# A graph network on one core: the first attention's weight product and its single-column vectors computed in two steps, with new hand-written orders

## The chip, the cores and the metric

The kernel runs on one core of one Trainium2 chip. The metric is the device time of one launch in microseconds (us); lower is better. The core's engines are PE (TensorE, matrix products), DVE (VectorE), ACT (ScalarE), POOL (GpSimd) and SP (SyncE, which only starts transfers). They run side by side, and each executes its own list of instructions strictly in order.

## The reference

Sixty-four graphs of 128 nodes with 256 features pass through four residual layers, each followed by a layer normalization:

```python
x = layernorm(x + attention(x, adj))      # L0: weight = adj * exp(q k^T), rows divided by their sums, times v
x = layernorm(x + gcn3(x, adj))           # L1: three times adj @ (x @ W) + b, relu after the first two
x = layernorm(x + hypergraph(x, adj))     # L2: up to 512, relu, layer norm, down to 256; H = (adj != 0)
x = layernorm(x + heads8(x, adj))         # L3: 8 heads, scores times 2*adj, softmax, Wo
```

Only the setup of L0 is changed. With q = x Wq^T + bq and k = x Wk^T + bk, the scores need, up to terms that the division by the row sums removes, the matrix Wq^T Wk, the vectors Wk^T bq and Wq^T bk, and the number bq . bk.

## The kernel before

**Groups.** Four graphs make a group; there are 16 groups. Each layer of a group is cut into named steps on each engine. For instance `att_t` multiplies the combined matrix "att" with the transposed input `xT`, `att_v0` and `att_v1` make the values, `att_scores` the scores, `att_exp` the exponentials, `att_turn` transposes them, and `att_out` multiplies with the values.

**The orders.** What runs when is written out by hand, in three tables with one list per engine. `PROLOGUE` fills the pipeline with groups 0 to 2. `SCHEDULE` is the loop, twelve iterations; in it, stage A is attention and GCN of group t, stage B the end of the GCN and the hypergraph layer of group t-1, stage C the eight heads of group t-2. `EPILOGUE` drains groups 13 to 15. Semaphores between the engines keep every order correct; an order only decides how long an engine stands at a wait. `keep_busy` steps on PE are four products of 512 columns whose result nobody reads.

**Split weights.** Every weight of a single-pass product is split by ACT into a rounded part (`high_W...`, line 978) and by DVE into what is left (`rest_W...`, line 1056: the weight minus its rounded part, both in SBUF). The input is split in the same way: `x_high` on ACT (line 906), `x_rest` on POOL (line 1382). All matrix products are recorded on line 476; one in full precision makes two records.

**The setup of L0.** `set_att` on PE waits for the biases and `Wq0`, `Wk0`. For each half m of the rows it makes the product (4 records of 256 columns) and behind it two vectors (8 records of one column); at the end comes bq . bk (4 records). Only then does it signal `att_mm`. `set_att` on DVE waits for that and for `Wv0T`, copies everything out of PSUM, and signals `att_ready`. ACT makes `high_att` from it, DVE `rest_att`, and PE's `att_t` waits for `rest_att`. `att_v0` waits for `rest_Wv0T`, whose last two columns hold one of the vectors. `att_t` on ACT adds the vector `t0`.

**Behind it on PE.** In `PROLOGUE`, `set_down` (16 records; waits for the transfer of `WdownT` and for DVE's `set_reps`) stands ahead of `att_t`, with two `keep_busy` steps ahead of it. DVE's `set_down` folds a gain into `WdownT`; ACT's `high_WdownT` waits for it.

**Transfers.** SP issues thirteen at the start: biases, `Wq0` and `Wk0`, `xT`, `Wv0T`, adjacency, x, rows, transposed adjacency, `W1` and `W2`, `W3` to `WoT`, `WdownT` (line 431), `WupT` with `Wqk3T` (line 432), and the adjacency once more.

**Steps of the loop that matter here.** `gram` on PE waits for the four sums `res0` that DVE's `att_out` and `att_res1` make. `hyper_down0` and `hyper_down1` on PE end with transposes of `sqs` (line 715), which DVE's `square_sum0` and `square_sum1` (lines 1216 to 1223) make. `z2_rest0` and `z2_rest1` on DVE (line 1147) subtract after ACT's `gcn_2a`. `hyper_out` on PE multiplies `y2`, which DVE makes in `hyper_y0` and `hyper_y1` (line 1228) after a power on POOL.

Of the kernel before, what the change touches and what calls it, by code (L numbers as in the profile page):

```python
# [1438 lines left out]
```

## Time and profile before

| | us |
|---|---|
| median of 3 runs | 1061.04 (1059.98 to 1061.5) |
| the profiled execution, its own time | 1061.14 |
| its span, first to last instruction | 1059.4 |
| mean granted clock of TensorE, share of full speed | 0.995 |

The profile is one execution. Durations are those of its records; "start" counts from the first instruction. In a list by time a row reads: start, length, engine, line, operation, output<-inputs, shapes, number of records merged in the row, and in brackets how long the engine had been idle and what ended that. PEld is the loading of weights into PE, which overlaps its products.

### The profile page before, as it was taken

Reading aid. Unit: us, or ns where it says so; the run is one execution under the profiler, and the core shown is the slowest. Engines: PE = TensorE matmul, PEld = TensorE weight load, DVE = VectorE, ACT = ScalarE, POOL = GpSimd, SP = SyncE. Lnnn points to the kernel's source line nnn. Section 1 sums busy time; section 2 is a strip of 40 time slices with the busy share of each in tenths; the row PEclk is TensorE's granted clock in tenths of the full one; section 3 lists DMA queues with packets and bytes.
Section 4 is the critical chain, followed back from the end, with each engine's and each line's share of the span. In section 5 each row is a group of like instructions: output and inputs, shape, how many; then the busy total and the mean of one; then the engine's idle time right before and its main releaser. Section 6 shows DMA issues by size and latency. Waiting matters only on the chain.

```text
span 1059.4 us, 21720 instructions
## 1 busy us (share of the span) xinstructions
PE 1026.7 (97%) x8376; PEld 913.4 (86%) x8376; DVE 839.8 (79%) x2247; ACT 654.5 (62%) x1755; POOL 485.2 (46%) x298
## 2 busy tenths in 40 slices
PE   8899999999999999999999999999999999998876
PEld 7688898898989889898988889898988989897764
DVE  4666878878797888879788887978888797978566
ACT  3444855839475683948568394856839485673724
POOL 2315363745435364543536464353546445351613
PEclk9999999999999999999999999999999999999998
DMA  6110101011110101111010111101011110000001
GB/s 228 50 61 9 62 2 61 21 41 51 33 59 21 51 21 41 51 41 50 22 50 22 40 51 41 51 21 50 31 32 51 41 51 21 32 2 11 21 1 40
DMA packets 17383, 43.35 MB, mean 41 GB/s; under 512 B 2048, under 2 KB 2048, under 8 KB 17152
## 3 DMA queue, kind: packets, MB, share of 16 engines
q1 hardware_dynamic: 17280, 41.97, 11.8%
q8 instruction: 66, 1.08, 0.4%
q14 instruction: 37, 0.30, 0.1%
HBM read 33.57 MB, written 8.39 MB: 40 GB/s over the span
## 4 chain that ended last, share of the span: by engine, by line
PE 92%; ACT 3%; DVE 3%; issue 1%; POOL 0%; DMA 0%; POOLq 0%; SPq 0%; DVEq 0%
PE ps L476 83%; PE ps L788 5%; PE ps L729 1%; ACT pr L948 1%; PE ps L579 1%; PE ps L715 1%; DVE pr L1245 1%; PE ps L659 1%; DMA pr<-in_weights 0%; DVE mx L1250 0%; DVE st L1067 0%; DVE aT_rest L1147 0%; ACT aT_high L885 0%; POOL rstd L1331 0%; ACT up_high L925 0%
## 5 line engine op out<-in xcount | busy, mean ns | idle before, releaser
L948 ACT ACTIVATE pr<-pr,mx 128x128 f32<-128x128 f32 x384 | 149.4, 407 | 9.6 <-DVE mx L1250 9.6
L1377 POOL TENSOR_TENSOR pr<-pr,den 128x1024 f32<-128x1024 f32 x64 | 122.1, 1916 | 56.6 <-DVE den L1265 56.6
L1331 POOL TENSOR_TENSOR rstd<-var,neg_half 128x4 f32<-128x4 f32 (+1 forms) x84 | 73.5, 876 | 143.9 <-DVE var L1078 143.9
L1083 DVE TENSOR_SCALAR x<-x,mv,rstd 128x256 f32<-128x256 f32 x256 | 90.6, 417 | 38.8 <-POOL rstd L1331 38.0
L1356 POOL TENSOR_TENSOR x<-x,rows 128x1024 f32<-128x1024 f32 x16 | 38.1, 2381 | 178.6 <-PE ps L476 178.6
L1067 DVE BATCH_NORM_STATS2 st<-x 128x6 f32<-128x256 f32 x256 | 91.6, 415 | 0.7
L1361 POOL TENSOR_TENSOR up_rest<-upT,up_high 128x1024 fp32r<-128x1024 f32 x32 | 81.9, 2561 | 0.0
L1245 DVE TENSOR_TENSOR pr<-ps,adjB 128x1024 f32<-128x1024 f32 x64 | 75.2, 1218 | 7.3 <-PE ps L476 7.3
L948 ACT ACTIVATION_READ_ACCUMULATOR pr<-pr,mx 128x1 f32 x384 | 79.1, 206 | 0.0
L902 ACT COPY s_s<-ps 128x512 f32<-128x512 f32 x32 | 18.8, 587 | 95.2 <-PE ps L476 95.2
L1250 DVE TENSOR_REDUCE mx<-pr 128x8 f32<-128x1024 f32 x64 | 76.4, 1201 | 0.0
L942 ACT ACTIVATE qkT<-ps,biases 128x512 f32<-128x512 f32 x64 | 42.2, 688 | 55.1 <-PE ps L476 54.9
L476 PE MATMUL ps<-W_high,aT_high 128*128 128x256 f32 x256 | 69.9, 298 | 1.9 <-ACT aT_high L885 1.9
L788 PE MATMUL ps<-ident,pr 128*128 128x128 f32 x512 | 67.6, 275 | 3.8 <-POOL pr L1377 1.9
L1366 POOL TENSOR_TENSOR hv<-hv,neg_half 128x2 f32<-128x2 f32 x32 | 22.4, 701 | 103.6 <-DVE hv L1211 103.6
L476 PE MATMUL ps<-W_rest,aT_high 128*128 128x256 f32 x256 | 65.6, 281 | 0.0
L788 PEld LDWEIGHTS ps<-ident,pr 128*128 128x128 f32 x512 | 57.5, 142 | 8.7 <-issue 5.7
L476 PE MATMUL ps<-WdownT_high,up_high 128*128 128x258 f32 x256 | 64.3, 283 | 0.0
L476 PE MATMUL ps<-WdownT_rest,up_high 128*128 128x258 f32 x256 | 63.9, 282 | 0.0
L1269 DVE COPY pr<-ps 128x512 f32<-128x512 f32 x64 | 43.5, 679 | 17.3 <-PE ps L788 17.0
L1350 POOL TENSOR_TENSOR x<-x,rows 128x1024 f32<-128x1024 f32 x16 | 38.6, 2413 | 38.7 <-PE ps L476 38.7
L1147 DVE TENSOR_TENSOR aT_rest<-ps,aT_high 128x512 fp32r<-128x512 f32 x64 | 41.7, 676 | 17.7 <-ACT ps L898 10.9
(199 smaller groups left out, 3310.7 us busy)
## 6 DMA issues: line engine op xcount, KB each, us to landing
xT<-in_xT SPq DMA_DIRECT2D x16, 512.0 KB, 3.7
x<-in_x SPq DMA_DIRECT2D x16, 512.0 KB, 3.3
out_x<-x SPq DMA_DIRECT2D x32, 256.0 KB, 2.1
adjA<-in_adj SPq DMA_DIRECT2D x16, 256.0 KB, 2.7
adjTA<-in_adjT SPq DMA_DIRECT2D x16, 256.0 KB, 2.7
adjB<-in_adj SPq DMA_DIRECT2D x16, 256.0 KB, 2.9
pr<-in_weights SPq DMA_DIRECT2D x2, 512.0 KB, 6.0
qkT<-in_weights SPq DMA_DIRECT2D x1, 1024.0 KB, 12.1
```

Of the source, the lines that this page charges most:

```text
L476: return pe.matmul(out, lhsT, rhs, start=(k == 0), stop=(k == n - 1))
L788: last = pe.transpose(ps4[:, turn_bank(b) + k // 4, k % 4], pr[:, b, k, :], ident[:])
L942: act.activation(qkT[:, m, :], ps[:, 4 + m, :], ACT.Identity, bias=b_qk[:, m, :], scale=ATT if m < C else 1.0).then_inc(qk_ready, 1)
L948: act.activation(pr[:, b, k, :], pr[:, b, k, :], ACT.Exp, bias=mx[:, b, k:k + 1], accum_out=den[:, b, 0, k:k + 1]).then_inc(exp_ready, 1)
L1067: dve.bn_stats(st[i][:, b, :], t[:, b, :]).then_inc(norm_step[i], 1)
L1083: dve.tensor_scalar(t[:, b, :], t[:, b, :], mv[i][:, b, 0:1], rstd[i][:, b:b + 1], ALU.subtract, ALU.mult).then_inc(ready, 1)
L1245: dve.tensor_tensor(pr[:, b].rearrange("p (j i) n -> p j i n", i=C), ps4[:, 4:8, 2 * bb:2 * bb + 2, :], mask, ALU.mult).then_inc(masked_re ...
L1250: dve.tensor_reduce(mx[:, b, :], pr[:, b], AX.X, ALU.max, negate=True).then_inc(mx_ready, 1)
L1269: dve.tensor_copy(pr[:, b, 4:8, :], ps4[:, turn_bank(b) + 1]).then_inc(prT_dve, 1)
L1331: pool.tensor_tensor(rstd[i][:, bs], var[i][:, bs], neg_half[:, bs], ALU.pow).then_inc(rstd_ready[i], len(pairs))
L1361: pool.tensor_tensor(up_rest[:, fs, :], upT[:, fs, :], up_high[:, fs, :], ALU.subtract).then_inc(up_rest_ready, 1)
L1377: pool.tensor_tensor(pr[:, b], pr[:, b], den[:, b, 1, :].unsqueeze(2).broadcast_to([P, HEADS, P]), ALU.mult).then_inc(pr_ready, 1)
```

## The change

1. **Two steps on PE.** `set_att` now makes only the two halves of the product and signals `att_mm` after each half. A new step `set_vec` makes the 20 single-column records, all into one bank of PSUM, and signals `vec_mm`.
2. **Two steps on DVE.** `set_att` copies each half when it is there (`att_ready` counts to 2). `set_vec` copies `t0` (now one copy of two columns), `c0` and the two columns of `Wv0T`, and signals `vec_ready`. `high_att` waits for `att_ready`; `high_Wv0T` and ACT's first `att_t` wait for `vec_ready`.
3. **Orders of the prologue.** ACT: `x_high` first, then `high_att`, `high_Wv0T`, `att_v0`; the other roundings later. PE: both first `keep_busy` ahead of `set_att`, `att_t` directly behind `set_vec`, `set_down` behind `att_v0`. DVE: `rest_att` and `rest_Wv0T` ahead of `set_reps`, `rest_W1` and `rest_W3` behind `gram_scale`, `rest_WoT` and `rest_Wqk3T` behind group 0. POOL: `x_rest0` ahead of `att_t` (the addition of the value bias to x).
4. **Orders of loop and epilogue.** Many neighbours change places on every engine. In all, PE has 5 instead of 7 `keep_busy` steps in the prologue and 12 instead of 10 in the epilogue.

```diff
 PROLOGUE = {
-    "PE": [("keep_busy2", 0), ("set_att", 0), ("keep_busy0", 0), ("keep_busy4", 0), ("set_down", 0), ("att_t", 0),
-        ("att_t_rest", 0), ("att_v0", 0), ("att_v1", 0), ("att_scores", 0), ("set_wo", 0), ("att_turn", 0),
+    "PE": [("keep_busy2", 0), ("keep_busy5", 0), ("set_att", 0), ("set_vec", 0), ("att_t", 0), ("att_t_rest", 0),
+        ("att_v0", 0), ("set_down", 0), ("att_v1", 0), ("att_scores", 0), ("set_wo", 0), ("att_turn", 0),
...
+        ("hyper_up01_rest", 0), ("hyper_up2", 0), ("gcn_ax", 1), ("hyper_up3", 0), ("gcn_1", 1),
+        ("gcn_1_rest", 1), ("hyper_down1_high", 0), ("hyper_down0_high", 0), ("gcn_2s1_high", 1), ("gcn_2s0_high", 1),
...
-    "DVE": [("set_rep", 0), ("set_att", 0), ("set_reps", 0), ("rest_WoT", 0), ("rest_att", 0), ("rest_Wv0T", 0),
-        ("set_down", 0), ("rest_W2", 0), ("incidence", 0), ("rest_WupT", 0), ("rest_Wv3T", 0), ("rest_W1", 0),
+    "DVE": [("set_rep", 0), ("set_att", 0), ("rest_att", 0), ("set_vec", 0), ("rest_Wv0T", 0), ("set_reps", 0),
+        ("incidence", 0), ("rest_W2", 0), ("rest_Wv3T", 0), ("set_down", 0), ("rest_WupT", 0), ("att_exp", 0),
...
-    "ACT": [("high_WoT", 0), ("high_Wv3T", 0), ("high_W2", 0), ("high_att", 0), ("high_Wv0T", 0), ("x_high", 0),
-        ("high_Wqk3T", 0), ("high_WupT", 0), ("high_WdownT", 0), ("high_W1", 0), ("att_v0", 0), ("att_t", 0),
+    "ACT": [("x_high", 0), ("high_att", 0), ("high_Wv0T", 0), ("att_v0", 0), ("high_W2", 0), ("high_Wv3T", 0),
+        ("high_WupT", 0), ("att_t", 0), ("att_v1", 0), ("att_off", 0), ("high_WdownT", 0), ("att_exp", 0),
...
-    "POOL": [("att_t", 0), ("x_rest0", 0), ("x0_stats0p", 0), ("x0_stats1p", 0), ("x_rest", 0), ("att_t", 1),
+    "POOL": [("x_rest0", 0), ("att_t", 0), ("x0_stats0p", 0), ("x0_stats1p", 0), ("x_rest", 0), ("x0_bias", 0),
...
@@ SCHEDULE, PE @@
-        ("B", "hyper_up01_rest"), ("B", "hyper_up3"), ("B", "hyper_up2"), ("A", "gcn_ax"), ("C", "mha_turn0"),
+        ("B", "hyper_up01_rest"), ("B", "hyper_up2"), ("B", "hyper_up3"), ("C", "mha_turn0"), ("A", "gcn_ax"),
...
@@ SCHEDULE, DVE @@
-        ("B", "square_sum0"), ("C", "mha_turn2"), ("C", "mha_turn3"), ("B", "square_sum1"), ("C", "x3_stats0"),
-        ("C", "mha_ctx1"), ("A", "z2_rest0"), ("C", "x3_norm0"), ("B", "hyper_down0"), ("C", "mha_wo1"),
+        ("C", "mha_turn2"), ("C", "mha_turn3"), ("C", "x3_stats0"), ("B", "square_sum0"), ("C", "mha_ctx1"),
+        ("A", "z2_rest0"), ("B", "square_sum1"), ("C", "x3_norm0"), ("C", "mha_wo1"), ("A", "z2_rest1"),
...
             def set_att(g):
                 pe.wait_ge(setup_in, 32)
                 for m in range(C):
                     for o in range(C):
-                        mm(ps[:, m, 0:D], wq0[:, o, m * P:(m + 1) * P], wk0[:, o, :], o, C)
+                        last = mm(ps[:, m, 0:D], wq0[:, o, m * P:(m + 1) * P], wk0[:, o, :], o, C)
+                    last.then_inc(att_mm, 1)
+
+            def set_vec(g):
+                pe.wait_ge(rep_ready, 1)
+                for m in range(C):
                     for o in range(C):
-                        mm(ps[:, m, D:D + 1], wk0[:, o, m * P:(m + 1) * P], bq0[:, o, :], o, C)
+                        mm(ps[:, 4, m:m + 1], wk0[:, o, m * P:(m + 1) * P], bq0[:, o, :], o, C)
                     for o in range(C):
-                        mm(ps[:, m, D + 1:D + 2], wq0[:, o, m * P:(m + 1) * P], bk0[:, o, :], o, C)
-                pe.wait_ge(rep_ready, 1)
+                        mm(ps[:, 4, C + m:C + m + 1], wq0[:, o, m * P:(m + 1) * P], bk0[:, o, :], o, C)
                 for o in range(C):
-                    last = mm(ps[:, 4, 0:1], rep(o), bk0[:, o, :], o, C)
-                last.then_inc(att_mm, 1)
+                    last = mm(ps[:, 4, 2 * C:2 * C + 1], rep(o), bk0[:, o, :], o, C)
+                last.then_inc(vec_mm, 1)
...
             def set_att(g):
-                dve.wait_ge(att_mm, 1)
+                for m in range(C):
+                    dve.wait_ge(att_mm, m + 1)
+                    dve.tensor_copy(w["att"][:, m, :], ps[:, m, 0:D]).then_inc(att_ready, 1)
+
+            def set_vec(g):
+                dve.wait_ge(vec_mm, 1)
                 dve.wait_ge(wv_in, 16)
-                dve.tensor_copy(c0[:], ps[:, 4, 0:1])
+                dve.tensor_copy(t0[:], ps[:, 4, 0:C])
+                dve.tensor_copy(c0[:], ps[:, 4, 2 * C:2 * C + 1])
                 for m in range(C):
-                    dve.tensor_copy(w["att"][:, m, :], ps[:, m, 0:D])
-                    dve.tensor_copy(t0[:, m:m + 1], ps[:, m, D:D + 1])
-                    last = dve.tensor_copy(w["Wv0T"][:, m, D:D + 1], ps[:, m, D + 1:D + 2])
-                last.then_inc(att_ready, 1)
+                    last = dve.tensor_copy(w["Wv0T"][:, m, D:D + 1], ps[:, 4, C + m:C + m + 1])
+                last.then_inc(vec_ready, 1)
```

## Rows read from the trace of the kernel before

**Rows 1.** The head of the page.

```profile
span 1059.4 us, 21720 instructions
```

**Rows 2.** Loop, epilogue: length; busy PE, PEld, DVE, ACT, POOL; granted clock; DMA share; GB/s.

```profile
161.30:898.44 737.14, 736.71 (x6194) 664.09 (x6193) 614.62 (x1646) 485.15 (x1308) 363.65 (x216) 1.00 0.12 40
898.44:1059.40 160.96, 138.72 (x1150) 116.79 (x1148) 117.81 (x287) 84.09 (x249) 60.11 (x40) 0.97 0.05 17
```

**Rows 3.** PE's list by time, start to the first group's scores.

```profile
1.51 2.07 PE L476 MATMUL ps<-fill 128*128 128x512 f32 x4 [1.51 <-DVE fill L1005]
...
5.31 2.08 PE L476 MATMUL ps<-pr 128*128 128x256 f32 x4 [1.72 <-DMA pr<-in_weights]
...
7.17 1.71 PE L476 MATMUL ps<-biases,pr 128*128 128x1 f32 x8
...
13.01 3.76 PE L476 MATMUL ps<-fill 128*128 128x512 f32 x8
...
16.57 4.58 PE L476 MATMUL ps<-pr,x 128*128 128x256 f32 x16
...
20.80 0.58 PE L476 MATMUL ps<-xT_high,att_high 128*128 128x512 f32 x1
...
27.07 2.05 PE L476 MATMUL ps<-xT,tT 128*128 128x128 f32 x16
...
35.87 2.10 PE L476 MATMUL ps<-fill 128*128 128x512 f32 x8
```

**Rows 4.** The issues of the last two weight transfers on SP, by time.

```profile
5.85 0.44 SPq L431 DMA_DIRECT2D pr<-in_weights  x1
...
6.33 0.45 SPq L432 DMA_DIRECT2D qkT<-in_weights  x1
```

**Rows 5.** Transfers issued before 8 us: size, time from issue to landing.

```profile
qkT<-in_weights SPq DMA_DIRECT2D x1, 1024.0 KB, 12.1
...
pr<-in_weights SPq DMA_DIRECT2D x1, 516.0 KB, 10.1
xT<-in_xT SPq DMA_DIRECT2D x1, 512.0 KB, 4.9
```

**Rows 6.** ACT, DVE and POOL by time, up to the first exponentials.

```profile
16.22 0.62 ACT L978 CAST att_high<-upT 128x512 fp32r<-128x512 f32 x1
...
16.87 0.69 DVE L1056 TENSOR_TENSOR att_rest<-upT,att_high 128x512 fp32r<-128x512 f32 x1
...
17.27 1.04 ACT L906 CAST xT_high<-xT 128x1024 fp32r<-128x1024 f32 x1
...
18.39 2.36 POOL L1382 TENSOR_TENSOR xT_rest<-xT,xT_high 128x1024 fp32r<-128x1024 f32 x1 [5.18 <-ACT xT_high L906]
...
25.74 1.28 ACT L851 ACTIVATE tT<-ps,t 128x512 f32<-128x512 f32 x2
...
29.16 1.14 ACT L867 ACTIVATE e_p<-ps,off 128x128 f32<-128x128 f32 x4 [0.77 <-PE ps L476]
```

**Rows 7.** DVE and POOL by time where a `rest_W...` meets POOL.

```profile
46.48 0.99 DVE L1056 TENSOR_TENSOR W_rest<-upT,W_high 128x512 fp32r<-128x512 f32 x1
...
46.87 2.84 POOL L1350 TENSOR_TENSOR x<-x,rows 128x1024 f32<-128x1024 f32 x1
```

**Rows 8.** What PE's weight loads waited for, 57.83 to 161.3 us: total, times, longest.

```profile
PEld ps L476 <- ACT aT_high L885: 1.6, 2, 1.3
PEld ps L476 <- ACT p0T L871: 1.4, 2, 0.9
```

**Rows 9.** The same in one iteration of the loop, 473.14 to 534.56 us.

```profile
PEld ps L476 <- DVE x L1129: 0.4, 1, 0.4
```

**Rows 10.** DVE and PE by time in the same iteration.

```profile
519.28 0.69 DVE L1147 TENSOR_TENSOR aT_rest<-ps,aT_high 128x512 fp32r<-128x512 f32 x1 [0.47 <-ACT ps L898]
...
520.58 0.38 PE L715 MATMUL ps<-ident,sqs 128*128 128x128 f32 x2
...
526.84 0.88 DVE L1228 SCALAR_TENSOR_TENSOR y<-ps,hv,r_down 128x256 f32<-128x256 f32 x2 [0.81 <-POOL hv L1366]
```

More of the change, by code:

```diff
@@ L62 @@
 PROLOGUE = {
-    "PE": [("keep_busy2", 0), ("set_att", 0), ("keep_busy0", 0), ("keep_busy4", 0), ("set_down", 0), ("att_t", 0),
-        ("att_t_rest", 0), ("att_v0", 0), ("att_v1", 0), ("att_scores", 0), ("set_wo", 0), ("att_turn", 0),
[4 rows of a table removed]
-        ("att_v0", 1), ("att_v1", 1), ("att_scores", 1), ("hyper_x", 0), ("att_turn", 1), ("att_out", 1),
[4 rows of a table removed]
-        ("gram_turn", 1), ("gcn_3s1", 1), ("att_t", 2), ("att_t_rest", 2), ("gcn_3a0", 1), ("mha_xt", 0),
[9 rows of a table removed]
-    "DVE": [("set_rep", 0), ("set_att", 0), ("set_reps", 0), ("rest_WoT", 0), ("rest_att", 0), ("rest_Wv0T", 0),
-        ("set_down", 0), ("rest_W2", 0), ("incidence", 0), ("rest_WupT", 0), ("rest_Wv3T", 0), ("rest_W1", 0),
-        ("rest_WdownT", 0), ("att_exp", 0), ("set_wo", 0), ("rest_Wqk3T", 0), ("att_out", 0), ("att_res1", 0),
[20 rows of a table removed]
@@ L107 @@
-    "ACT": [("high_WoT", 0), ("high_Wv3T", 0), ("high_W2", 0), ("high_att", 0), ("high_Wv0T", 0), ("x_high", 0),
-        ("high_Wqk3T", 0), ("high_WupT", 0), ("high_WdownT", 0), ("high_W1", 0), ("att_v0", 0), ("att_t", 0),
-        ("att_v1", 0), ("high_W3", 0), ("att_off", 0), ("att_exp", 0), ("att_turn", 0), ("gcn_ax", 0), ("x_split", 0),
-        ("gcn_1", 0), ("gcn_2s0", 0), ("gcn_2s1", 0), ("gcn_2a", 0), ("gcn_3s0", 0), ("gcn_3s1", 0), ("gram_turn", 0),
-        ("att_t", 1), ("att_v0", 1), ("att_v1", 1), ("att_off", 1), ("att_exp", 1), ("att_turn", 1), ("hyper_x", 0),
[10 rows of a table removed]
@@ new lines @@
+    "DVE": [("set_rep", 0), ("set_att", 0), ("rest_att", 0), ("set_vec", 0), ("rest_Wv0T", 0), ("set_reps", 0),
+        ("incidence", 0), ("rest_W2", 0), ("rest_Wv3T", 0), ("set_down", 0), ("rest_WupT", 0), ("att_exp", 0),
[22 rows of a table added]
+        ("high_WupT", 0), ("att_t", 0), ("att_v1", 0), ("att_off", 0), ("high_WdownT", 0), ("att_exp", 0),
+        ("high_WoT", 0), ("att_turn", 0), ("high_W3", 0), ("high_W1", 0), ("gcn_ax", 0), ("gcn_1", 0), ("gcn_2s0", 0),
+        ("gcn_2s1", 0), ("x_split", 0), ("gcn_2a", 0), ("gcn_3s0", 0), ("gcn_3s1", 0), ("high_Wqk3T", 0),
+        ("gram_turn", 0), ("att_v0", 1), ("att_t", 1), ("att_v1", 1), ("att_off", 1), ("att_exp", 1), ("hyper_x", 0),
[16 rows of a table added]
@@ L130 @@
+    "SP": [("att_turn", 0), ("att_out", 0), ("att_scores", 0), ("gcn_3a1", 0), ("att_scores", 1), ("att_out", 1),
+        ("att_turn", 1), ("gcn_3a1", 1), ("att_scores", 2), ("att_turn", 2), ("att_out", 2), ("mha_scores1", 0),
         ("x3_norm0", 0), ("x3_norm1", 0)],
@@ L818, in _ @@
             run(pe, "PE", {
-                "set_att": set_att, "set_down": set_down, "set_wo": set_wo,
+                "set_att": set_att, "set_vec": set_vec, "set_down": set_down, "set_wo": set_wo,
                 **{f"keep_busy{i}": keep_busy for i in range(16)},
@@ L848, in att_t @@
             def att_t(g):
+                if first(g):
+                    act.wait_ge(vec_ready, 1)
                 for m in range(C):
@@ L972, in step @@
                     elif name == "att":
-                        act.wait_ge(att_ready, 1)
+                        act.wait_ge(att_ready, C)
                     else:
@@ L1282, in _ @@
                 **{f"mha_sum{b}": lambda g, b=b: mha_sum(g, b) for b in WHOLE},
-                "set_rep": set_rep, "set_reps": set_reps, "set_att": set_att, "set_down": set_down, "set_wo": set_wo,
+                "set_rep": set_rep, "set_reps": set_reps, "set_att": set_att, "set_vec": set_vec, "set_down": set_down, "set_wo": set_wo,
                 **{f"rest_{name}": set_rest(name) for name in PARTED},
```

9 lines of the change are left out of this document (4 added, 5 removed), and 248 rows, old and new, of tables (EPILOGUE, PROLOGUE, SCHEDULE).

## The prediction

> **What bounds the kernel now.** I read the stretches of the three tables first. In the loop PE is busy for 736.71 of 737.14 us [rows 2]; twelve iterations in that time make 61.4 us each, and nothing but fewer or denser products could shorten them much. The epilogue has PE busy for 138.72 of 160.96 us [rows 2]. So an early start of the first group is worth its full length to the end: once the pipeline is filled, everything hangs on PE. Then PE's own list from the start [rows 3]: the inputs of `set_att` are there at 5.31, but the first product of the first group starts at 20.80 and its scores at 27.07. Between them stand work that the scores don't need at once (`set_down`, from 16.57) and eight filler products that only cover a wait (3.76 us from 13.01). The lists of ACT and DVE show what was waited for: the combined matrix was rounded only at 16.22 and its remainder made at 16.87 [rows 6], far behind the products of `set_att`, because the copy waited for all vectors and ACT had other weights first.
>
> **TensorE's clock in this stretch.** The same four-product filler took 2.07 us at 1.51, eight took 3.76 from 13.01, but eight took 2.10 from 35.87 [rows 3]. So PE works at the lower of its two levels (1.2 GHz) until some time in `set_down`, and at 2.4 GHz behind it. One pass of 512 cycles is thus near 0.45 us early and 0.23 to 0.26 us later (an estimate from these rows). `set_down` took 4.23 us from start to next step, partly at the low level; all at the high one I take 16 x 0.23 = 3.7.
>
> **The first group, step by step.** Fillers: two, from 1.5 to about 5.2, in time that was waiting anyway; cost nothing, since `set_att` can't start ahead of 5.31. Their cover is the landing of the first weights.
>
> `set_att`: 8 passes at 0.26 to 0.47 us, so done between 7.4 and 9.1; I take 8.5, for the denser start should bring the high clock earlier than the broken-up one before, but not at once. Then DVE's copy (one cast of the same half size is below 0.62), ACT's rounding 0.62 and DVE's remainder 0.69 [rows 6]: 8.5 + 0.2 + 0.4 + 0.6 + 0.7 = 10.4 for `rest_att`. `set_vec`: 20 records of one column; eight took 1.71 us at the low clock [rows 3], so 4.2 us there, near 2.1 at the high one: it ends between 10.6 and 12.9. `att_t` starts then, 8 to 10 us ahead of 20.80. The rounded input is in time: `xT` lands 4.9 us after its issue as third transfer, near 6.6 (estimate: the eleventh is issued at 5.85 [rows 4, 5]); `x_high` takes 1.04 and `x_rest0` 2.36 us [rows 6], so both are there at about 10.0.
>
> `att_t` with its rest is twelve passes of 512 columns, 3.0 us at 0.25, `att_v0` twelve of half the width, 1.5 more: PE is through at 15.1 to 17.4. Now `set_down` wants `WdownT`, issued at 5.85 and 10.1 us under way [rows 4, 5]: 15.95. That transfer, not the clock, is the floor: early clock or late, `set_down` starts between 16.0 and 17.4 and ends near 19.7 (upper case 21.1). `att_v1` adds 1.5 us: 21.2. The other way in is the addition of `t0` on ACT. In the new order it stands behind `high_WupT`, whose transfer lands at 6.33 + 12.1 = 18.4 [rows 4, 5]; rounding it takes 1.04 (the size of the `x_high` row), the addition 1.28 [rows 6]: 20.8. Both ways meet: scores at 21.2 against 27.07, **5.9 us earlier**; lower bound 4.5 (low clock throughout `set_vec` and a late `set_reps`), upper 6.2. The exponentials start at 29.16 because of the scores; in the new order `high_WdownT` stands ahead of them and is ready at about 23 (an estimate: the fold, five operations of at most 0.4 us on DVE, behind `set_down`'s 19.7, then 1.04 on ACT), just when the scores are. I let the 5.9 stand.
>
> **A rule against it.** DVE took 0.99 us for a `rest_W...` that elsewhere takes 0.69, and POOL's addition beside it 2.84 us [rows 6, 7]; POOL's addition began 0.39 us into the DVE row, when the operation ahead of it on POOL was done. The new order puts `x_rest0` (POOL, to about 10.0) beside `rest_att` and the bias addition (about 10.8 to 13.1, when the rows have landed) beside `rest_Wv0T`. If each waits for the other's end, `att_t` starts at about 10.9, `rest_Wv0T` is done at 13.8 and `set_reps` near 15.9. The Trainium skill, "SBUF — State Buffer", section "Who interferes with whom", says that a DVE instruction with two SBUF inputs and a POOL one that reads SBUF exclude each other for the whole instruction; the rows agree. By it the scores would still be at 21.2, since the waits end ahead of the landing at 15.95; without it the sum is the same.
>
> **The rest of the prologue.** (a) `rest_W1` and `rest_W3` stand between `gram_scale` and the remainders of the first `gcn_ax`, and a filler stands ahead of `gcn_2s0`: 0.1 + 0.15 us lost; bounds 0 and 1.4 (two of 0.69). (b) In group 1 PE waited for ACT behind `gcn_1_rest`, at most 1.3 us at once [rows 8]. The new order has two `hyper_down` steps there, so 0.9 us of it goes. (c) Behind `att_turn` of group 1 PE waited 0.9 us at most for `p0T` [rows 8]. ACT now makes the two copies of `hyper_x` first: 0.5 us more. (d) In group 2 ACT does `att_turn` ahead of a value copy and with four exponentials fewer in front: 0.5 us less. (e) The larger number of switches between kinds of products: nothing to 0.4 us, I take 0.2. Sum (a) to (e): 0.4 to 0.5 gained; with the start 6.3 us.
>
> **The loop.** The same products, so only waits can change. PE's loads waited 0.4 us an iteration for DVE's `res0` sums (`gram`) [rows 9], of which about 0.15 us delays PE; `att_res1` now runs ahead of `hyper_rest0`, so this goes. `mha_turn0` comes ahead of `gcn_ax`, sixteen passes of 128 columns (2.05 us for as many [rows 3]); its buffers are free because the four `up_out` steps run ahead of one set of exponentials. Against that, `square_sum1` now stands behind `z2_rest0`, which starts at 519.28 when ACT is done [rows 10]. It makes its two sums at 519.9 to 521.3; the transposes that need them run at 520.58 before [rows 10] and at 521.5 in the new order (`mha_wo1`, eight passes of 256 columns, 1.0 us, now ahead of `hyper_down0`). That holds by 0.2 us. The last `y2` stay at 526.84 to 527.7 [rows 10], since POOL's power follows the end of `hyper_down1`; that caps what PE can gain. I take 0.05 us less an iteration, 0.6 in all; bounds from 0.15 gained (1.8) to 0.5 lost (6).
>
> **The epilogue.** Its waits are chains through exponentials, powers and remainders that keep their links. The two more fillers stand in waits. `up_out3` behind `exp2a` costs about 0.3 us in group 14, the order behind the last `hyper_out` returns about as much; the last group's first division comes 0.7 us later behind an `x3_norm1`, of which 0.2 reaches the end. Net 0.2 lost, bounds 1.5 either way: the granted clock is 0.97 there [rows 2], and where it dips is partly chance.
>
> **The sum.** 6.3 + 0.6 - 0.2 = 6.7 us. Against the profiled execution: span 1059.4 [rows 1] becomes 1052.7; its own time, 1061.14, has 1.7 us around the span and becomes 1054.4. The median of the runs is 1061.04, 0.1 below it. I predict 1054.4. What this measurement can tell from no change is 0.2%, 2.1 us.
>
> **Rivals.** (1) The loop gains too: the waits at `gram` and `mha_turn1` fall away in full, 0.15 to 0.3 us an iteration, 1051 to 1053. For it: DVE has slack, 614.62 of 737.14 us [rows 2]; against it: the `y2` chain. Chance 0.15. (2) The start gains less: `set_vec` at the low clock, or a clock that falls behind it because one-column products and the wait for `rest_att` are little work. Price 1 to 2 us, so 1055.5 to 1057. The Trainium skill, "TensorE: Matmul & The Clock Gate", section "What's actually happening", says that recent activity sets the clock; by it either could happen. Chance 0.2. (3) The loop loses a little: 0.2 to 0.4 us an iteration at a new DVE wait, 1057 to 1059.5. Chance 0.15. (4) Slower: the two sums of `square_sum1` come too late for line 715, each iteration. They would do this if ACT's `gcn_2a`, now behind `squares1` and the `mha_ctx1` copy, slips. It loses what it slips beyond 0.2 us, times twelve; from (6.7 + 2.1)/12 = 0.73 us an iteration on the kernel is slower, for instance 1.0 us: 1066. Chance 0.05. (5) No change: the transfers or `set_reps` hold the first group back and the 5.9 shrink to 2 or less, or case 3 reaches 0.5 us: about 1060. Chance 0.07. The forecast has the rest, 0.38, own range 1053.3 to 1055.5.
>
> **How the numbers follow.** Faster by over 0.2% (below 1058.9) are the forecast, cases 1 and 2, and most of case 3: 0.38 + 0.15 + 0.2 + 0.13 = 0.86. The same: case 5 and the end of case 3, 0.08. Slower: case 4 and 0.01 for two small losses at once, 0.06. From 1051.0 to 1059.0 leaves out the best end of case 1 and cases 4 and 5, under 2 in 10.
>
> **What would show it.** In the new trace: product of `set_att` in one piece from 5.3; first product with the rounded input near 11 to 13; `set_down` from 16.0; scores at 21.2; exponentials near 23; the loop 737 us long or up to 1 less, without the wait of rows 9. The prediction is wrong if the loop's PE shows a wait of some tenths at line 715 or at the products with `y2`, or if the scores start behind 23.

## The result, and the profile after

| | before | after |
|---|---|---|
| median, us | 1060.51 (4 runs, 1059.52 to 1061.5) | 1052.26 (4 runs, 1051.77 to 1052.53) |
| ratio, 95% interval | | 0.9926 [0.9913, 0.9938] |
| span of the profiled execution | 1059.4 | 1049.6 |

The change makes the kernel 0.74% faster by the ratio; the medians differ by 8.25 us. The forecast was 1054.4, 6.7 us less than the profiled execution of the kernel before; the profiled spans differ by 9.8. The measured median is inside the stated range (1051.0 to 1059.0), but 1.0 us below the lower end of the forecast's own range (1053.3 to 1055.5), where the prediction had placed its first rival. The head of the page after:

```profile
span 1049.6 us, 21721 instructions
```

The windows view of prologue, loop and epilogue; the columns are those of [rows 2]:

```profile
0.00:153.69 153.69, 143.25 (x1028) 126.66 (x1029) 110.75 (x316) 85.20 (x198) 60.56 (x42) 1.00 0.20 71
153.69:889.80 736.11, 734.55 (x6194) 665.05 (x6193) 611.34 (x1645) 484.34 (x1309) 363.64 (x216) 1.00 0.12 40
889.80:1049.60 159.80, 139.55 (x1158) 117.76 (x1156) 122.54 (x286) 84.12 (x249) 61.46 (x40) 0.97 0.05 18
```

Against [rows 2] the loop begins 7.6 us earlier (153.69, 161.30), is 1.0 us shorter (61.34 us an iteration, 61.42 before) and the epilogue 1.2 us shorter. PE's list by time at the start, to be read against [rows 3] (its line L475 was L476 before):

```profile
1.51 3.78 PE L475 MATMUL ps<-fill 128*128 128x512 f32 x8 [1.51 <-DVE fill L1010]
5.21 2.16 PE L475 MATMUL ps<-pr 128*128 128x256 f32 x8
7.21 1.84 PE L475 MATMUL ps<-biases,pr 128*128 128x1 f32 x16
...
10.63 0.50 PE L475 MATMUL ps<-xT_high,att_high 128*128 128x512 f32 x1 [1.13 <-DVE att_rest L1065]
...
15.85 3.72 PE L475 MATMUL ps<-pr,x 128*128 128x256 f32 x16 [0.48 <-DMA pr<-in_weights]
...
20.84 1.95 PE L475 MATMUL ps<-xT,tT 128*128 128x128 f32 x16
```

`set_att` is one piece of 2.16 us, 0.25 us a pass, so PE is at its higher level for nearly all of it: the record of the granted clock begins at 5.58 with 1.00, in the kernel before at 18.52. (Ahead of the first record the windows view counts 1.00, though the eight filler products there took 3.78 us, the length of the lower level.) `att_t` starts 10.2 us earlier, `set_down` starts when `WdownT` has landed, and the scores start 6.23 us earlier. The other engines by time, against [rows 6]:

```profile
6.48 1.04 ACT L911 CAST xT_high<-xT 128x1024 fp32r<-128x1024 f32 x1 [4.47 <-DMA xT<-in_xT]
7.68 2.35 POOL L1391 TENSOR_TENSOR xT_rest<-xT,xT_high 128x1024 fp32r<-128x1024 f32 x1 [6.07 <-ACT xT_high L911]
...
8.52 2.06 DVE L1065 TENSOR_TENSOR att_rest<-upT,att_high 128x512 fp32r<-128x512 f32 x1 [0.68 <-ACT att_high L983]
...
10.65 2.39 POOL L1346 TENSOR_TENSOR x<-x,rows 128x1024 f32<-128x1024 f32 x1 [0.62 <-DMA rows<-in_rows]
...
11.59 2.00 DVE L1065 TENSOR_TENSOR Wv0T_rest<-pr,Wv0T_high 128x516 fp32r<-128x516 f32 x1 [0.75 <-ACT Wv0T_high L983]
...
18.32 1.04 ACT L983 CAST WupT_high<-qkT 128x1024 fp32r<-128x1024 f32 x1 [1.46 <-DMA qkT<-in_weights]
19.27 1.26 ACT L856 ACTIVATE tT<-ps,t 128x512 f32<-128x512 f32 x2
...
22.83 1.14 ACT L872 ACTIVATE e_p<-ps,off 128x128 f32<-128x128 f32 x4
```

The two remainders on DVE took 2.06 and 2.00 us instead of 0.69. Each ended 0.55 us after POOL's instruction beside it (10.03 and 13.04). What PE's weight loads waited for in one iteration of the loop, against [rows 9]:

```profile
PEld ps L475 <- DVE pr L1278: 0.4, 1, 0.4
PEld ps L475 <- DVE gm L1204: 0.3, 1, 0.3
```

The wait of [rows 9] for the sums ahead of `gram` is gone. A new one stands at `gcn_1`, put down to DVE's `gm`; who really ends it is a question of experiments 8 and 12. In experiment 12 one disturbed execution counts in the median and not in the ratio; without it the median is 1051.8.

### The profile page after: what moved, and what is told of

It is laid out like the page before. It is cut to its first block, busy times and chain, and to the rows that moved or that the text cites. A ratio compares the mean times of both kernels' runs of the same rounds, so it can differ in the third digit from the quotient of the medians.

```text
span 1049.6 us, 21721 instructions
## 1 busy us (share of the span) xinstructions
PE 1017.4 (97%) x8376; PEld 909.5 (87%) x8376; DVE 844.6 (80%) x2246; ACT 653.7 (62%) x1755; POOL 485.7 (46%) x298
## 4 chain that ended last, share of the span: by engine, by line
PE 90%; ACT 5%; DVE 2%; issue 1%; DMA 1%; POOL 0%; SPq 0%; POOLq 0%; DVEq 0%
PE ps L475 82%; PE ps L791 5%; ACT pr L953 1%; PE ps L732 1%; DMA pr<-in_weights 1%; ACT up_high L930 1%; ACT upT L933 1%; PE ps L718 1%; DVE pr L1254 1%; PE ps L662 1%; PE ps L582 1%; ACT fT_high L926 0%; DVE st L1076 0%; DVE mx L1259 0%; DVE x L1138 0%
## 5 line engine op out<-in xcount | busy, mean ns | idle before, releaser
L1340 POOL TENSOR_TENSOR rstd<-var,neg_half 128x4 f32<-128x4 f32 (+1 forms) x84 | 78.1, 930 | 117.0 <-DVE var L1087 117.0
L1365 POOL TENSOR_TENSOR x<-x,rows 128x1024 f32<-128x1024 f32 x16 | 38.7, 2418 | 182.4 <-PE ps L475 182.4
L1370 POOL TENSOR_TENSOR up_rest<-upT,up_high 128x1024 fp32r<-128x1024 f32 x32 | 76.8, 2402 | 2.6 <-ACT upT L933 2.6
L475 PE MATMUL ps<-W_high,aT_high 128*128 128x256 f32 x256 | 70.8, 302 | 2.4 <-ACT aT_high L901 1.4
L475 PE MATMUL ps<-WdownT_high,up_high 128*128 128x258 f32 x256 | 66.3, 291 | 0.0
L475 PE MATMUL ps<-W_rest,aT_high 128*128 128x256 f32 x256 | 65.5, 281 | 0.0
L475 PE MATMUL ps<-WdownT_rest,up_high 128*128 128x258 f32 x256 | 64.0, 282 | 0.0
L475 PE MATMUL ps<-fT_high,WupT_high 128*128 128x512 f32 x128 | 53.6, 419 | 0.7 <-ACT fT_high L926 0.7
```

Source lines behind the costliest of these rows:

```text
L475: return pe.matmul(out, lhsT, rhs, start=(k == 0), stop=(k == n - 1))
L1340: pool.tensor_tensor(rstd[i][:, bs], var[i][:, bs], neg_half[:, bs], ALU.pow).then_inc(rstd_ready[i], len(pairs))
L1370: pool.tensor_tensor(up_rest[:, fs, :], upT[:, fs, :], up_high[:, fs, :], ALU.subtract).then_inc(up_rest_ready, 1)
```

## Experiments

The table has the ratio to the kernel before, run beside each, and landmarks of the one profiled execution of each kernel, in us: start of the first scores, start of the loop, length of the loop, length of the epilogue to the end of the span.

| kernel | median us | ratio [95%] | scores | loop from | loop | epilogue |
|---|---|---|---|---|---|---|
| before | 1060.51 | 1 | 27.07 | 161.3 | 737.1 | 161.0 |
| after | 1052.26 | 0.9926 [0.9913, 0.9938] | 20.84 | 153.7 | 736.1 | 159.8 |
| 1 new prologue alone | 1055.05 | 0.9951 [0.9938, 0.9963] | 21.70 | 156.1 | 737.3 | 159.7 |
| 2 old loop | 1054.1 | 0.9943 [0.9929, 0.9957] | 20.98 | 153.9 | 737.2 | 160.9 |
| 3 old epilogue | 1052.99 | 0.9932 [0.9918, 0.9946] | 21.58 | 156.0 | 736.0 | 159.6 |
| 4 one filler less | 1054.23 | 0.9947 [0.9933, 0.9961] | 22.04 | 154.9 | 736.1 | 160.9 |
| 5 `set_down` first | 1063.12 | 1.0024 [1.0014, 1.0033] | 30.18 | 165.8 | 735.8 | 159.9 |
| 6 setup in one step | 1057.13 | 0.9968 [0.9956, 0.998] | 25.35 | 158.3 | 735.9 | 159.8 |
| 7 POOL waits | 1053.26 | 0.9938 [0.9925, 0.9951] | 21.89 | 154.7 | 735.7 | 159.8 |
| 8 `gcn_ax` first in the loop | 1051.93 | 0.9926 [0.9914, 0.9938] | 20.93 | 155.1 | 735.7 | 159.8 |
| 9 `set_down` late | 1052.71 | 0.9932 [0.9919, 0.9945] | 18.41 | 154.4 | 735.9 | 161.0 |
| 10 late, in halves | 1054.11 | 0.995 [0.9932, 0.9968] | 15.54 | 155.5 | 736.0 | 159.8 |
| 11 as 10, fold moved | 1049.5 | 0.9899 [0.9882, 0.9915] | 16.11 | 150.8 | 736.0 | 160.6 |
| 12 as 11, loop with `gcn_ax` first, `degrees` moved | 1051.97 | 0.9915 [0.9899, 0.9931] | 15.66 | 150.4 | 736.1 | 159.8 |

### 1 to 3: which part of the change gives what

```diff
 # 1: the new prologue and its code, the other two tables of before
-SCHEDULE, EPILOGUE of after
+SCHEDULE, EPILOGUE of before
 # 2: after with SCHEDULE of before     # 3: after with EPILOGUE of before
```

> The new prologue (its code, orders of all engines) in front of the old loop and the old epilogue. If the three parts add up as the two traces read, the prologue ends 7.6 us earlier, the loop stays at 737.1 us (61.42 each iteration) and the epilogue at its old length: span near 1051.8, time near 1053.4, 7.1 below the kernel before. Rival: the later half of the gain needs the new loop's order; then the prologue gives 5 us or less, 1055.5 or more.

> The changed kernel with the old loop. Theory: the wait at the products of gram goes with the new order and most of it comes back behind mha_turn1, which leaves 0.08 us an iteration. So the old loop has 61.42 us again instead of 61.34, costs 1.0 us and gives 1053.2. Rival: the 0.08 are not the loop's order but what the earlier start leaves over; then an iteration stays at 61.34 and the time at 1052.3.

> The changed kernel with the old epilogue. Theory: the old filler keep_busy6 of the last group stands ahead of mha_turn3 in a stretch where the granted clock is half, and runs longer than the wait it covers; this costs 1.2 us: 1053.4, with mha_turn3 about 9.9 us behind mha_turn1 instead of 8.3. Rival: where the clock falls is chance of one execution; then the median is 1052.3 and the epilogue's gain is nothing.

Run 1, the first products of its setup in PE's list, then the windows view of two stretches of its prologue and of its epilogue:

```profile
5.49 2.99 PE L475 MATMUL ps<-pr 128*128 128x256 f32 x8 [0.20 <-DMA pr<-in_weights]
...
10.02 0.58 PE L475 MATMUL ps<-biases,x 128*128 128x1 f32 x4
```

```profile
10.95:14.36 3.41, 3.41 (x8) 2.73 (x9) 2.66 (x8) 0.62 (x1) 2.34 (x1) 0.50 1.03 424
48.49:51.91 3.42, 3.42 (x16) 3.42 (x17) 0.00 (x0) 0.59 (x1) 3.42 (x2) 0.50 0.00 0
...
893.39:1053.10 159.71, 137.49 (x1150) 115.30 (x1148) 117.78 (x287) 84.10 (x249) 60.04 (x40) 0.99 0.05 18
```

The time missed the sum by 1.6 us. The same prologue that reached the loop at 153.69 in the changed kernel reached it at 156.11 here: the granted clock was 0.50 in two stretches in which it was 1.00 there. `att_t` took 3.52 us instead of 1.95, and the two `gcn_3s` steps at 48.5 took 3.5 instead of 2.0. The clock also rose later: its record begins at 7.53 instead of 5.58, and `set_att` took 2.99 us instead of 2.16. Run 3 shows all of this too (record from 7.61, loop from 155.97), run 8 the second stretch alone (record from 6.42, loop from 155.12), run 2 neither (5.85, 153.85); all four have one and the same list of instructions up to the loop. So the loop's order doesn't decide it: of the two with the old loop one shows both stretches and one none, and so do run 3 and the changed kernel with the new one. Measured against the changed kernel, the scores came 0.74 and 0.86 us later in runs 3 and 1, and the second stretch cost 1.3 to 1.6 us more. Without both the profiled execution of run 1 (1055.26) would lie at 1052.9, within 0.6 of the sum. That it is chance of the execution is the plain reading, but it isn't shown: only one execution of each kernel was profiled, and all five of run 1 took 1054.6 to 1055.4 us, so none of them was as fast as the sum.

Run 2: the loop is 737.19 us long again. All three profiled executions with the old loop have 737.1 to 737.3, the nine with the new one 735.7 to 736.1. So the loop's order gives 1.0 to 1.6 us, on average 1.2, or 0.1 us an iteration; that much is shown. The median, 1054.1, is 0.9 above the theory; its five times spread from 1052.9 to 1055.7. Run 3 and the epilogue, windows view:

```profile
155.97:891.96 735.99, 734.44 (x6194) 664.98 (x6193) 611.34 (x1645) 484.41 (x1309) 363.35 (x216) 1.00 0.12 40
891.96:1051.60 159.64, 138.65 (x1150) 116.32 (x1148) 117.78 (x286) 84.14 (x249) 60.01 (x40) 0.97 0.05 18
```

The old epilogue took 159.7 us in run 1 and 159.6 in run 3, against 161.0 in the trace of before; the new one 159.8 to 159.9 in seven executions and 160.6 to 161.0 in four. The expected 1.2 us for it did not come: my theory, that the old filler is badly placed, fell. The median of run 3 is 0.7 us above that of the changed kernel, which its interval covers. What differs is where the clock falls. The windows view of run 2, with the new epilogue, from 1043.50:

```profile
1043.50:1051.90 8.40, 2.46 (x12) 2.17 (x11) 3.35 (x12) 0.00 (x0) 0.70 (x1) 0.50 0.17 62
```

From 1043.50 on the last `mha_wo1` ran at half clock and took 1.91 us instead of 1.10; the changed kernel's own profile had its low stretch from 1019.34 to 1026.17 and the last products at 1.00.

### 4 to 6: what the start gains by

```diff
 # 4
-    "PE": [("keep_busy2", 0), ("keep_busy5", 0), ("set_att", 0), ...
+    "PE": [("keep_busy2", 0), ("set_att", 0), ... ("keep_busy0", 0), ("keep_busy5", 0), ("gcn_ax", 0), ...
 # 5 (on DVE set_reps moves ahead of rest_att)
-    "PE": ... ("set_vec", 0), ("att_t", 0), ("att_t_rest", 0), ("att_v0", 0), ("set_down", 0), ...
+    "PE": ... ("set_vec", 0), ("set_down", 0), ("att_t", 0), ("att_t_rest", 0), ("att_v0", 0), ...
 # 6: one signal, behind the last vector product
-                    last.then_inc(att_mm, 1)
...
-                last.then_inc(vec_mm, 1)
+                last.then_inc(att_mm, C)
...
-                    dve.wait_ge(att_mm, m + 1)
+                    dve.wait_ge(att_mm, C)
```

> The changed kernel with one filler instead of two ahead of set_att (the other stands behind gram). Theory A: eight fillers without a break are what brings the granted clock up by 5.6 us; without the second the products of set_att, set_vec and some of att_t run at the lower level, att_v0 ends behind the landing of WdownT (15.8 us), and the scores start at 22 to 24 us instead of 20.84: 1053.5 to 1056. Theory B: the landing of WdownT is the floor and hides it; the scores stay within 0.5 us of 20.84 and the time at 1052.3.

> The changed kernel with set_down back ahead of att_t on PE (and set_reps ahead of rest_att on DVE, so that set_down finds its vectors); the setup in two steps and all else stay. Theory: the place of set_down behind the landing of WdownT is what the start gains by. att_t then waits for the end of set_down, 19.2 us or later, and the scores start at 25.4 or later instead of 20.84: 1056.8 or more, up to 1059 if the empty time from 9.5 to 15.8 lets the granted clock fall. Rival: the two steps are what counts; then it stays below 1054.5.

> The changed kernel with the same products in the same order, but one signal behind all of them: DVE copies the combined matrix only when the single-column vectors are done too. Theory: the copies start at 9.5 instead of 7.4, rest_att is done near 11.9 instead of 10.57, att_v0 ends near 16.7, and most of that is hidden by the landing of WdownT at 15.8: scores 0.5 to 1.0 us later, 1052.9 to 1053.3. Rival: the step in two is worth its full 2.1 us at the scores: 1054.4.

Run 4, PE's list by time:

```profile
1.51 2.07 PE L456 MATMUL ps<-fill 128*128 128x512 f32 x4 [1.51 <-DVE fill L991]
5.62 3.68 PE L456 MATMUL ps<-pr 128*128 128x256 f32 x8 [2.04 <-DMA pr<-in_weights]
```

With a pause of 2.04 us behind the filler, `set_att` took 3.68 us, not 2.16; the record of the granted clock begins at 9.08 and has 0.50 from 12.49 to 15.90. Scores 1.2 us later, time in the range of theory A. In the twelve profiled executions with eight filler products ahead of `set_att` the record of the clock begins between 4.89 and 7.61, so the second filler does bring the higher level earlier. The landing hides part of the loss only. How much of the 1.2 us is the filler and how much the low stretch, one execution can't say.

Run 5, PE's list, and the windows view of its low stretch:

```profile
16.16 6.12 PE L434 MATMUL ps<-pr,x 128*128 128x256 f32 x16 [5.59 <-DMA pr<-in_weights]
```

```profile
10.81:21.05 10.24, 4.89 (x12) 3.91 (x13) 7.16 (x20) 0.62 (x1) 2.42 (x1) 0.50 0.72 297
```

This is slower than the kernel before, with a setup in two steps and rounded x ahead: PE waits 5.59 us for `WdownT`, the clock falls at 10.81, `set_down` takes 6.12 us instead of 3.72, and `att_t` starts at 21.93. I expected scores from 25.4 on and up to 1059; it is 30.18 and 1063. Besides the clock, PE waited 2.1 us ahead of the scores for `tT`, since the value copies and three roundings stand ahead of it on ACT. So the place of `set_down` carries the start: with these two things that follow from it, it costs 9.3 us at the scores, more than the whole gain.

Run 6, DVE and POOL by time, and the windows view:

```profile
11.00 2.34 POOL L1345 TENSOR_TENSOR x<-x,rows 128x1024 f32<-128x1024 f32 x1 [0.66 <-DMA rows<-in_rows]
11.14 2.74 DVE L1064 TENSOR_TENSOR att_rest<-upT,att_high 128x512 fp32r<-128x512 f32 x1 [0.68 <-ACT att_high L982]
```

```profile
11.93:18.76 6.83, 4.83 (x11) 3.80 (x12) 6.05 (x20) 0.62 (x1) 1.40 (x1) 0.50 0.94 390
```

Both expectations fell: without the step in two the scores come 4.5 us later, and the median is 4.9 us higher. The copies started 2.3 us later than the second one had, so `rest_att` now met POOL's second instruction, which began 0.14 us ahead of it, and took 2.74 us; PE idled from 9.66 to 13.94, the clock fell at 11.93, and `att_t` with its rest and `att_v0` took 6.5 us instead of 4.7. What the landing was to hide had grown past it. Only the 2.3 us are the step's own; the rest is what it ran into.

### 7: the remainders beside POOL

```diff
             def x_rest(g):
+                if first(g):
+                    pool.wait_ge(rest_ready["att"], 1)
...
             def att_t(g):
                 if first(g):
                     pool.wait_ge(rows_in, 16)
+                    pool.wait_ge(rest_ready["Wv0T"], 1)
```

> The changed kernel; POOL waits for rest_att before its subtraction x_rest0, and for rest_Wv0T before its first addition to x. Theory: DVE's rest_att took 2.05 us and rest_Wv0T 2.00 us because POOL was at work on SBUF beside them; alone they take 0.7. att_t then starts at 9.5 instead of 10.63, but WdownT still lands at 15.8, so the scores stay at 20.8 and the time at 1052.3 (within 0.5). Rival: DVE's rows stay at 2.0 us, the 2 us being something else (their landing, their wait for ACT).

DVE, POOL and PE by time:

```profile
8.81 0.69 DVE L1065 TENSOR_TENSOR att_rest<-upT,att_high 128x512 fp32r<-128x512 f32 x1 [0.68 <-ACT att_high L983]
...
12.72 2.48 DVE L1028 TENSOR_SCALAR x<-mean_mat,biases 128x128 f32<-128x128 f32 x1
12.73 2.38 POOL L1347 TENSOR_TENSOR x<-x,rows 128x1024 f32<-128x1024 f32 x1 [0.69 <-issue]
...
16.92 1.32 PE L475 MATMUL ps<-pr,x 128*128 128x256 f32 x5 [2.17 <-DVE x L1030]
```

`rest_att` alone took 0.69 us and `att_t` started at 9.66: shown, the 2.06 came from the POOL instruction beside it. But the stall only moved. `rest_Wv0T` now met POOL's subtraction (9.65 to 12.05) and took 1.66 us. POOL's addition stood beside `set_reps`, held one of its scalings for 2.48 us (0.27 otherwise), and `set_down` waited for them until 16.92: scores 1.05 us later. The Trainium skill, "SBUF — State Buffer", section "Who interferes with whom", has both forms: two inputs in SBUF, or a scaling in a two-port mode. The trace agrees.

### 8: what holds the loop

```diff
-    "PE": ... ("C", "mha_turn0"), ("A", "gcn_ax"), ("C", "mha_turn1"), ...
+    "PE": ... ("A", "gcn_ax"), ("C", "mha_turn0"), ("C", "mha_turn1"), ...
```

> The changed kernel with one step of the loop moved back: PE makes gcn_ax ahead of mha_turn0, not behind it. In the changed kernel only mha_turn1 stands between the end of gcn_ax and gcn_1, which waits for ACT's copies of its result: 0.35 us an iteration. Theory: with both turns between them this wait goes, and gcn_ax waits instead up to 0.3 us for DVE's normalised rows: from 0.35 us less to 0.1 us more an iteration, 1048.5 to 1053.5, most likely 1050.5. Rival: the iteration is set by another chain (the y2 rows behind hyper_down1, POOL's powers) and stays at 61.34 us: 1052.3.

The iteration was 61.30 to 61.33 us, as the rival had it; the median, 1051.93, can't be told from that of the changed kernel. The wait behind `mha_turn1` shrank by 0.25 us, and 0.24 came back ahead of and inside `gcn_ax`. One iteration of the changed kernel, PE and ACT by time, up to the first product of `gcn_1`, and the windows view of the 12 us around it; last, the windows view of the whole loop in run 8:

```profile
492.96 1.95 PE L475 MATMUL ps<-adjTA,x 128*128 128x128 f32 x16
494.75 1.04 PE L791 MATMUL ps<-ident,pr 128*128 128x128 f32 x8
495.16 1.10 ACT L885 CAST aT_high<-ps 128x512 fp32r<-128x512 f32 x2
495.92 0.47 PE L475 MATMUL ps<-aT_high,W_high 128*128 128x512 f32 x1
```

```profile
484.50:496.50 12.00, 11.87 (x73) 10.27 (x72) 11.51 (x38) 11.87 (x39) 7.45 (x5) 1.00 0.20 66
```

```profile
155.12:890.86 735.74, 735.74 (x6195) 664.27 (x6194) 611.15 (x1645) 483.99 (x1309) 363.17 (x216) 1.00 0.12 40
```

In this loop PE is never idle by its records (735.74 of 735.74 us), so what is left to gain there without fewer or denser products is small.

### 9 to 12: a start that doesn't wait for `WdownT`

```diff
 # 9, PE (ACT: att_t ahead of att_v0, high_WupT behind att_exp; the fold and its roundings later)
-    ("att_v0", 0), ("set_down", 0), ("att_v1", 0), ... ("gram", 0), ("keep_busy0", 0), ("gcn_ax", 0), ...
+    ("att_v0", 0), ("att_v1", 0), ... ("gram", 0), ("set_down", 0), ("gcn_ax", 0), ...
 # 10: halves; DVE makes x_rest0 ahead of rest_att; POOL's first addition waits for rest_Wv0T
+    "PE": ... ("gram", 0), ("set_down0", 0), ("gcn_ax", 0), ... ("gcn_2a", 0), ("set_down1", 0), ...
+    "DVE": ... ("x1_norm1p", 0), ("set_down", 0), ("rest_WoT", 0), ("incidence", 1), ("att_exp", 1), ...
 # 11
+    "PE": ... ("gcn_1_rest", 0), ("set_down1", 0), ("gcn_2s0_high", 0), ... ("gcn_2a", 0), ("keep_busy4", 0), ...
+    "DVE": ... ("z1_rest1", 0), ("set_down", 0), ("z2_rest0", 0), ... ("gcn_ax1", 1), ("rest_WdownT", 0), ...
 # 12, loop: PE gcn_ax ahead of mha_turn0, and
-    "DVE": ... ("A", "degrees"), ("A", "x0_stats"), ("C", "mha_max3"), ("A", "x0_norm"), ...
+    "DVE": ... ("A", "x0_stats"), ("C", "mha_max3"), ("A", "x0_norm"), ("A", "degrees"), ...
```

> The changed kernel with set_down taken out of the way of the first scores: PE makes it behind gram, in the place of the filler keep_busy0, which moves ahead of gcn_1_rest; its fold on DVE, the rounding and the remainder of WdownT follow later; on ACT the addition of t0 stands ahead of the value copies and the rounding of WupT behind the exponentials. Theory: the landing of WdownT (15.8 us) is what holds the scores at 20.84 now; without it the chain product, rounding, remainder, att_t sets them, at 17.0. set_down takes 3.7 us where the filler took 2.1, so gcn_ax starts 2.3 us earlier than at 31.66: 1049.5 to 1050.3. If the clock falls in more executions than before, up to 1.5 more. Rival: another landing or the weights' rounding on ACT holds the exponentials back, and no more than 1 us is gained: 1051.3 or more.

> As the run before it, with three more steps: set_down in two halves, one behind gram and one behind gcn_2a, where PE waited 1.7 us for ACT; DVE instead of POOL makes the first remainder of the rounded x, ahead of rest_att; POOL's first addition to x waits for rest_Wv0T. Theory: no POOL instruction on SBUF is then beside rest_att or rest_Wv0T, which take 0.7 us instead of 2; att_t starts near 9.8 instead of 10.63, the scores near 16.0 instead of 20.84, and both halves of set_down lie in waits: 4.0 to 4.8 us less than the changed kernel, 1047.5 to 1048.3. Rival: the waits that set_down fills were set by chains that move with it (DVE's fold, POOL's later addition to x, the residual that needs it), and less than 3 us is gained.

> As the run with set_down in two halves, with the places of what follows it mended: the second half behind gcn_1_rest (a filler takes its place behind gcn_2a), its fold on DVE behind z1_rest1, where DVE waited for ACT for some us, the rounding of WdownT behind att_turn of group 1 and its remainder behind the remainders of that group's gcn_ax. Theory: the 3.2 us that the first group of the run before had gained at att_t of group 1 were lost because DVE made the fold ahead of incidence and the masking of group 1 (PE waited 3.0 us for it); with the fold in DVE's empty time they stay: loop from 150.5, 3.2 less than the changed kernel, 1048.8 to 1049.5. Rival A: POOL's long additions hold DVE's fold or the masking up again, and less than 2 us stays: 1050.3 or more. Rival B: the granted clock falls in most executions (as at 59.96 us in the run before) and takes 1 to 3 us of it.

> The best kernel so far (set_down in halves, fold in DVE's empty time) with two steps of the loop moved: PE makes gcn_ax ahead of mha_turn0, and DVE makes the degrees behind the scaling of x0 instead of ahead of its statistics. Theory: with gcn_ax first PE waited 0.14 us at the end of hyper_up3 and 0.10 inside gcn_ax for DVE's scaled rows, and that alone kept the iteration at 61.31; the four small operations of the degrees (0.65 us) stand in that chain. Behind it they delay nobody, because gram_scale ends as before: 61.05 to 61.15 us an iteration, 2 to 3 us less than the run before: 1046.5 to 1047.5. Rival: POOL's power or another chain of the period (remainders, y2) sets the iteration, and the wait comes back elsewhere on PE: 61.3 and 1049.5.

Run 9 gained 2.4 us at the scores, not 3.8 (`att_t` lay in a low stretch from 11.71 to 15.13), and gave all but 0.4 back at `gcn_ax` (31.24), since `set_down` took 3.46 us in the filler's place: 1052.7 us, nothing gained, as its rival said. Still it shows that the landing of `WdownT` is what holds the scores of the changed kernel. Run 10 went by its theory up to `att_t` of group 1 (48.36, 3.2 earlier), lost it behind that and ended at 1054.1, slower than the changed kernel by 1.9 us where 4.0 to 4.8 less was expected. PE's waits from 50 to 66 us, then DVE and POOL by time:

```profile
PE ps L529 <- DVE e_p L1082: 3.0, 1, 3.0
```

```profile
53.90 1.65 DVE L1000 SCALAR_TENSOR_TENSOR pr<-pr,biases,ps 128x256 f32<-128x256 f32 x4
...
58.10 2.65 POOL L1319 TENSOR_TENSOR x<-x,rows 128x1024 f32<-128x1024 f32 x1 [5.22 <-PE ps L420]
58.47 3.04 DVE L1082 TENSOR_TENSOR e_p<-e_p,adjA 128x128 f32<-128x128 f32 x4
```

The fold at 53.90 pushed the masking of group 1 (the multiplication of `e_p` with `adjA`) under POOL's next addition: its four operations took 3.04 us, where three took 0.81 in the changed kernel. The clock was at 0.50 from 59.96 to 66.78 besides; how the loss splits between the two, one execution can't say. Run 11 puts the fold where DVE waited for ACT. DVE by time, and the windows view of the prologue:

```profile
36.14 1.29 DVE L1109 TENSOR_TENSOR aT_rest<-ps,aT_high 128x512 fp32r<-128x512 f32 x2 [3.68 <-ACT ps L841]
37.34 0.41 DVE L998 COPY r_down<-ps 128x256 f32<-128x256 f32 x1
37.68 1.65 DVE L1000 SCALAR_TENSOR_TENSOR pr<-pr,biases,ps 128x256 f32<-128x256 f32 x4
...
43.39 1.29 DVE L1109 TENSOR_TENSOR aT_rest<-ps,aT_high 128x512 fp32r<-128x512 f32 x2 [3.85 <-ACT ps L852]
```

```profile
0.00:150.82 150.82, 142.97 (x1028) 126.68 (x1029) 112.20 (x317) 84.94 (x198) 59.43 (x41) 1.00 0.21 73
```

Its gain stays: the loop begins 2.9 us earlier than in the changed kernel, 1049.5 us as expected, and it has the best ratio here, though its interval touches that of the changed kernel. Run 12 tells about the loop: PE and ACT by time, in the iteration of the rows above:

```profile
488.81 1.95 PE L398 MATMUL ps<-adjTA,x 128*128 128x128 f32 x16
490.59 1.91 PE L718 MATMUL ps<-ident,pr 128*128 128x128 f32 x16
491.87 1.11 ACT L812 CAST aT_high<-ps 128x512 fp32r<-128x512 f32 x2
492.63 0.47 PE L398 MATMUL ps<-aT_high,W_high 128*128 128x512 f32 x1
```

Its critical chain from 460 to 521 us is PE's own work but for one piece, in which PE waited for nothing that the profile shows:

```profile
492.50 0.13 issue
```

The waits for the scaled rows are gone, as its theory had it, and the iteration is still 61.31 to 61.37, the rival. ACT casts the result of `gcn_ax` 1.1 us after its last product (490.76), because it is at its exponentials until then; in the changed kernel it was busy for 11.87 of the 12 us around the first product of `gcn_1`. In the changed kernel and in runs 8 and 12 the first product of `gcn_1` came 0.14 us behind the end of the first cast, but 0.35, 0.36 and 0.25 us behind `gm`: the profile named the wrong engine. So at this place ACT's own list sets the pace, and an earlier product only waits longer. It is a small pace: the idle time of PE in the chain is 0.13 us an iteration. No run moved the cast ahead of the exponentials, so what that would give is open. Five runs of this kernel fell in two groups, 1048.0 and 1048.1 at a granted clock of 0.995, 1051.8 to 1052.2 at 0.991 to 0.992: chance of the clock is as large here as the step that was tried.

## Why the prediction was right

- **Floor of the start: right.** `set_down` at 15.85 (forecast 15.95 to 16.0), `tT` ready at 20.5 (20.8), scores at 20.84 (21.2), exponentials at 22.83 (near 23). 6.23 us were gained where 5.9 stood. Run 5 shows that the place of `set_down` carries this, and run 9 that the landing of `WdownT` holds the rest.
- **The clock at the start: the forecast fits one execution and not another.** `set_att` was to end at 8.5 and ended at 7.4, `set_vec` at 9.5 and not between 10.6 and 12.9 (by the prediction's own terms, 8.5 and 4.2, the upper end is 12.7). But in run 1, with the same list, they ended at 8.5 and 10.6. I had put the rise of the clock down to the denser start of `set_att`; the second filler does it too (run 4: record from 9.08 without it, from 4.89 to 7.61 with it). It mattered little, since POOL's instruction held `rest_att` until 10.6 or 10.8 in both, and behind that `set_down` waits for the landing.
- **The rule on DVE and POOL: it held,** with `att_t` at 10.63 (10.9), `rest_Wv0T` done at 13.59 (13.8) and `set_reps` at 15.56 (near 15.9), and the scores still came at the landing, as the sum by the rule said. Run 7 shows the lock and run 6 what it costs when nothing hides it.
- **Rest of the prologue: right in (b), (c), (d), too low in sum.** (b) 0.98 us gained (0.9), (c) 0.54 lost (0.5), (d) 0.47 gained (0.5). The losses (a) and (e), 0.45 together, did not come, and some waits of 0.1 to 0.2 us went that I hadn't listed. 7.6 us instead of 6.3.
- **The loop: way right, half the size, cap wrong.** 0.1 us an iteration for 0.05. The wait at `gram` went (0.25) and 0.20 at `mha_turn0`; 0.35 came back behind `mha_turn1`, since only one turn now covers the cast. The prediction named the `y2` rows as the cap; PE never waited for them. What was won ahead of `gcn_1` came back as a wait for ACT's cast of `gcn_ax`'s result (runs 8 and 12), and beyond that PE's own products are the cap, as the prediction's first paragraph had it: in run 8 they fill the loop. What ACT's list in turn waits for, over a whole iteration, was not followed. `square_sum1`, the rival on the slow side, showed no wait.
- **The epilogue: neither shown nor refuted.** 0.2 lost was forecast, the profile shows 1.2 gained; but in runs 1 and 3 the old epilogue takes 159.6 to 159.7, so the 1.2 us can't be put down to the new order, and 0.2 us is less than these runs can tell.
- **The sum.** By runs with the old and the new parts the new prologue gives 7.6 us where the clock stays up and 5.2 to 6.2 where it falls, the loop's order 1.2, the epilogue's nothing that these runs can tell. The forecast was 1.3 short in the first and 0.6 in the second. The kernel before was profiled once, in an execution of 1061.14 us, while its medians beside the experiments were 1059.8 to 1060.7; part of each difference can be that execution's.
- **What was luck.** The time, 1052.26, lies in the range of the first rival (1051 to 1053), but not by its cause: that asked for 0.15 to 0.3 us an iteration, and the loop gave 0.1. Of the 1.3 us that the prologue gave beyond the forecast, 0.3 came at the scores and the rest in the waits of groups 1 and 2. With the clock as in the profile of run 1 the same list would have come out about 2.4 us later (an estimate from the two prologues), near the forecast. So how close the number came is in part chance of the clock.

## What to carry to other kernels

First find the transfer that lands last, and keep whatever needs it out of the list ahead of what doesn't; then look where the engine that waits meanwhile loses its clock. A stall on DVE beside a long POOL instruction need not go when POOL is moved; in run 7 it met the next operations. See what stands beside it then, and try giving the work to DVE (run 10: `att_t` at 9.61) or putting it beside operations that read PSUM. Before believing in a difference of 1 or 2 us between two profiles, compare the granted clock over time, its first rise too; compare the length of a part over all executions that have it in common.
